# A decoder layer on one core: the scan's output projection as three products of split operands, its weight streamed

## The reference

```python
proj = hidden_states @ W_in.T
z, xBC, dt = split(proj)
xBC = silu(conv4(xBC) + conv_b)
dt = softplus(dt + dt_bias)
A_cum = cumsum(dt * -exp(A_log))
Lmat = exp(segsum(dA))
y = Y_diag + Y_off + D * x
g = y * silu(z)
gn = g * rsqrt(mean(g * g) + EPS) * norm_w
return gn @ W_out.T
```

## Time and profile before

| what | value |
|---|---|
| median of three runs | 1694.83 us |
| profiled execution, its own time | 1693.64 us |
| its span | 1691.9 us |
| TensorE matmul busy | 1603.2 us (95%) |
| VectorE busy | 1254.0 us (74%) |
| ScalarE busy | 1217.1 us (72%) |
| GpSimd busy | 731.8 us (43%) |
| mean DMA rate | 134 GB/s |

### The profile page before, as it was taken

One profiled execution on the slowest core, in us unless ns is written; L12 is line 12 of the kernel. 1 busy time (PEld: TensorE's weight loads), 2 busy tenths in 40 slices (PEclk: granted clock), 3 DMA queues, 4 the chain that ended last, 5 costly groups with the idle time before them and its releaser, 6 DMA issues. The chain is left out here.

```text
span 1691.9 us, 29098 instructions
## 1 busy us (share of the span) xinstructions
PE 1603.2 (95%) x9864; PEld 1281.0 (76%) x9864; DVE 1254.0 (74%) x2044; ACT 1217.1 (72%) x2518; POOL 731.8 (43%) x601
## 2 busy tenths in 40 slices
PE   5479999999999999999999999999969999999999
PEld 3357777777777777777777677878757889999888
DVE  7969999999999999999999865567666533333355
ACT  4679999999999999999999576566624324444331
POOL 1425555555555555555555511311113653334460
PEclk9689999999999999999999999999989999999999
DMA  8966444444444444444444100000215323222231
GB/s 324 389 231 253 164 152 172 150 158 167 151 172 152 154 171 150 173 151 153 172 150 150 55 1 13 14 14 14 72 75 190 117 96 133 90 91 95 79 99 51
DMA packets 78078, 226.62 MB, mean 134 GB/s; under 512 B 9072, under 2 KB 32880, under 8 KB 76272
## 3 DMA queue, kind: packets, MB, share of 16 engines
q1 hardware_dynamic: 72272, 198.67, 32.9%
q0 software_dynamic: 5664, 26.09, 4.4%
HBM read 187.77 MB, written 36.96 MB: 133 GB/s over the span
## 5 line engine op out<-in xcount | busy, mean ns | idle before, releaser
L776 DVE SCALAR_TENSOR_TENSOR m_xc<-banks,k_cw,m_xc 128x510 f32<-128x510 f32 (+2 forms) x384 | 285.4, 743 | 16.6 <-ACT m_xc L690 7.2
L917 PE MATMUL m_ps_out<-k_won,m_gT 128*128 128x256 f32 x1024 | 242.3, 379 | 3.2 <-POOL m_gT L640 2.0
L873 PE MATMUL banks<-pair_hi,m_wxz 128*128 128x512 f32 x680 | 241.7, 406 | 2.5 <-DMA m_wxz<-w_split 2.5
L640 POOL TENSOR_TENSOR m_gT<-m_gy,m_zs 128x512 f32<-128x512 f32 x128 | 166.4, 1300 | 172.3 <-DVE m_gy L817 171.4
L663 POOL TENSOR_TENSOR m_mat<-m_mat,k_cbm 128x384 f32<-128x384 f32 x128 | 129.8, 1014 | 230.6 <-DVE m_mat L789 216.8
L917 PEld LDWEIGHTS m_ps_out<-k_won,m_gT 128*128 128x128 f32 x1024 | 193.6, 190 | 36.1 <-POOL m_gT L640 3.3
L905 PE MATMUL m_ps_y<-m_mat,m_xdt 128*64 128x256 f32 (+1 forms) x2048 | 194.7, 332 | 0.0
L711 ACT ACTIVATE m_mat<-m_mat 128x1536 f32<-128x1536 f32 x128 | 188.6, 1473 | 0.0
L905 PEld LDWEIGHTS m_ps_y<-m_mat,m_xdt 128*64 128x64 f32 x2048 | 126.8, 136 | 80.0 <-issue 42.3
L702 ACT ACTIVATE m_mat<-m_a_all,k_cum 128x256 f32<-128x256 f32 x340 | 170.6, 502 | 0.0
L651 POOL TENSOR_TENSOR m_g_sum<-m_g_sum,m_g_sq 128x512 f32<-128x512 f32 x124 | 162.4, 1310 | 5.3 <-ACT m_g_sq L717 5.1
(11 more groups left out here) (325 smaller groups left out, 3774.9 us busy)
## 6 DMA issues: line engine op xcount, KB each, us to landing
m_wxz<-w_split SPq DMA_DIRECT2D x85, 512.0 KB, 3.4
m_a_all<-a_by_head SPq DMA_DIRECT2D x85, 512.0 KB, 4.4
k_w_first<-w_split SPq DMA_DIRECT2D x43, 512.0 KB, 3.3
k_a_first<-a_by_head SPq DMA_DIRECT2D x43, 512.0 KB, 4.2
w_split<-p_w_hl SPq DMA_DIRECT2D x15, 1024.0 KB, 8.6
raw<-in_w_gate_up POOLq DMA_DIRECT2D x9, 1280.0 KB, 6.5
raw<-in_w_xz SPq DMA_DIRECT2D x16, 512.0 KB, 7.1
raw<-in_w_down POOLq DMA_DIRECT2D x9, 640.0 KB, 7.9
```

The costliest lines, as they stand in the source:

```text
L640: pool.tensor_tensor(gT[:, n % 2, :], gy[:, n % 2, :], zs[:, n % 2, :], ALU.mult).then_inc(g_done, 1)
L776: dve.scalar_tensor_tensor(out=out[:, :, k:], in0=ps[:, :, 0:SEQ - k], scalar=cw[:, c, TAPS - 1 - k:TAPS - k], in1=out[:, :, k:], op0=ALU. ...
L873: last = pe.matmul(ps[:, :], w, a, start=m == 0, stop=m == len(terms) - 1)
L917: last = pe.matmul(ps_out[:, q * HID:(q + 1) * HID], gT[:, n % 2, q * P:(q + 1) * P], won[:, c, :], start=c == 0 and q % 2 == 0, stop=c == ...
```

## The change

The output projection no longer multiplies float32 operands. Each product g is split into a high part (`gT_hi`, ScalarE) and a low part (`gT_lo`, GpSimd) of type float32r, the output weight likewise (`won[..., 0]` and `won[..., 1]`), and `out_proj` issues three matmuls for each of the four token tiles: high x high, high x low, low x high, 12 in all. It runs one iteration later, for n-2 instead of n-1.

The output weight is no longer loaded in preparation. In the first group each tile of it is loaded (128 KB), multiplied by norm_w and rounded on ScalarE (`won_high`), its low part taken on VectorE (`won_low`), and the pair stored to DRAM (256 KB). In the later groups the pair is loaded again for each product, four buffers deep. All of that is issued by SyncE's queue (`move_won`).

One of the four pairs of `gaps` (head 1, sequence 1) moves from ScalarE to GpSimd (`pool_gaps`), three products ahead; `decays` now also waits for it. The sign that ScalarE took in `scale=-1.0` is now in the stored sums. Several semaphores are merged under new names (`x_silu` and `z_silu` to `silu_done` and so on), with counts to match.

```diff
-            def weigh_out(c):
-                if c == 0:
-                    act.wait_ge(wo_loaded, 16)
-                act.activation(won[:, c, :], won[:, c, :], ACT.Copy, scale=nw[:, c:c + 1]).then_inc(won_done, 1)
...
-            sp.dma_start(won[:], w_out).then_inc(wo_loaded, 16)
...
+            def move_won(n):
+                kept_c, c = n - WON - 2, n - WON
+                if n > WON:
+                    sp.wait_ge(won_moved, 16 * won_moves(n - 1))
+                if 0 <= kept_c < NCT:
+                    sp.wait_ge(won_lo_done, kept_c + 1)
+                    sp.dma_start(won_dram[kept_c], won[:, kept_c % WON].rearrange("p s m -> p (s m)").bitcast(F32))\
+                        .then_inc(won_moved, 16)
+                if 0 <= c < NCT:
+                    if c >= WON:
+                        sp.wait_ge(won_lo_done, c - WON + 1)
+                    sp.dma_start(won_raw[:, c % WON], w_out[:, c, :]).then_inc(won_moved, 16)
+                elif c >= NCT:
+                    sp.wait_ge(out_ready, c - WON + 1)
+                    sp.dma_start(won[:, c % WON].rearrange("p s m -> p (s m)").bitcast(F32), won_dram[c % NCT])\
+                        .then_inc(won_moved, 16)
...
-                    sp.wait_ge(gap_done, HPT * (n - 2))
+                    sp.wait_ge(exp_done, n - 2)
...
+            def low_part(n):
+                pool.wait_ge(gT_hi_done, n + 1)
+                if n >= 2:
+                    pool.wait_ge(out_ready, n - 1)
+                pool.tensor_tensor(gT_lo[:, n % 2, :], gT[:, n % 2, :], gT_hi[:, n % 2, :].bitcast(F32),
+                                   ALU.subtract).then_inc(gT_lo_done, 1)
...
+            def pool_gaps(n):
+                g, c, u = n // NCT, n % NCT, n % 3
+                pool.wait_ge(a_loaded[u], 16 * (n // 3 + 1))
+                if n >= 3:
+                    pool.wait_ge(y_ready, n - 2)
+                h, b = HPT - 1, BG - 1
+                head, t = c * HPT + h, g * TPG + 2 * b
+                pool.tensor_scalar(mat[:, u, h, b * TRI:b * TRI + SEQ], a_all[u][:, h, b * SEQ:(b + 1) * SEQ],
+                                   cum[:, t, head:head + 1], 0.0, ALU.add, ALU.max)
+                pool.tensor_scalar(mat[:, u, h, b * TRI + SEQ:(b + 1) * TRI],
+                                   a_all[u][:, h, b * SEQ + P:(b + 1) * SEQ],
+                                   cum[:, t + 1, head:head + 1], 0.0, ALU.add, ALU.max).then_inc(mat_pool, 1)
...
                     pool.wait_ge(mat_done, HPT * (n + 2))
                     last_matrix(n + 1)
+                if n >= 1:
+                    low_part(n - 1)
                 if n < N - 1:
                     product(n)
+                if n + 3 < N:
+                    pool_gaps(n + 3)
                 if n % NCT > 0:
                     add_square(n - 1)
...
-                for b in range(BG):
+                for b in range(BG - h):
...
             def decays(n):
                 act.wait_ge(gap_done, HPT * (n + 1))
+                act.wait_ge(mat_pool, pool_gap(n))
                 act.activation(mat[:, n % 3], mat[:, n % 3], ACT.Exp, scale=-1.0).then_inc(exp_done, 1)
+
+            def high_part(n):
+                act.wait_ge(g_done, n + 1)
+                if n >= 2:
+                    act.wait_ge(out_ready, n - 1)
+                act.activation(gT_hi[:, n % 2, :], gT[:, n % 2, :], ACT.Copy).then_inc(gT_hi_done, 1)
+
+            def won_high(c):
+                act.wait_ge(won_moved, 16 * won_moves(c + WON))
+                if c >= WON:
+                    act.wait_ge(out_ready, c - WON + 1)
+                act.activation(won[:, c % WON, 0], won_raw[:, c % WON], ACT.Copy, scale=nw[:, c:c + 1])\
+                    .then_inc(won_hi_done, 1)
...
-                if n == N - 1:
-                    wq_high()
-                if n >= 1:
-                    square(n - 1)
+                high_part(n - 1)
+                square(n - 1)
                 if n + 1 < N:
                     tanh_z(n + 1)
                 if n + 2 < N:
                     decays(n + 2)
+                if n <= NCT:
+                    won_high(n - 1)
+                if n == N - 1:
+                    wq_high()
+            high_part(N - 1)
             square(N - 1)
...
+            def won_low(c):
+                dve.wait_ge(won_hi_done, c + 1)
+                dve.scalar_tensor_tensor(out=won[:, c % WON, 1], in0=won_raw[:, c % WON], scalar=nw[:, c:c + 1],
+                                         in1=won[:, c % WON, 0].bitcast(F32), op0=ALU.mult, op1=ALU.subtract)\
+                    .then_inc(won_lo_done, 1)
...
                     silu_x(n + 1)
                     silu_z(n + 1)
+                if 1 <= n <= NCT:
+                    won_low(n - 1)
...
+                terms = [(gT_hi, 0), (gT_hi, 1), (gT_lo, 0)]
                 for q in range(TPG):
-                    last = pe.matmul(ps_out[:, q * HID:(q + 1) * HID], gT[:, n % 2, q * P:(q + 1) * P],
-                                     won[:, c, :], start=c == 0 and q % 2 == 0, stop=c == NCT - 1,
-                                     skip_group_check=True)
+                    for m, (a, part) in enumerate(terms):
+                        last = pe.matmul(ps_out[:, q * HID:(q + 1) * HID], a[:, n % 2, q * P:(q + 1) * P],
+                                         won[:, n % WON, part], start=c == 0 and q % 2 == 0 and m == 0,
+                                         stop=c == NCT - 1 and m == len(terms) - 1, skip_group_check=True)
```

162 lines of the change are left out of this document (95 added, 67 removed).

## The result

The changed kernel takes **1853.31 us** (median of four runs, 1852.20 to 1856.42) against 1694.60 us for the kernel before on the same chip: 1.0945 times as long, with a 95% interval of 1.0931 to 1.0958. The forecast was 1755, its range 1733 to 1788. The direction and both loops were right; the result lies 98 us above the forecast and 65 above the range.

The account below looks back on a forecast made before the run. The kernel was taken as bound by TensorE, 6.57 us per product. First group +40, groups two to four +20, preparation -1, tail +2 made +61 on 1693.64, 1754.6, given as 1755 us; range 1733 to 1788.

Parts of the forecast that it names:

- both loops: The first group's loop through `won_high` and `won_low`, 7.91 us, and the GpSimd-VectorE port loop in groups two to four, 6.78 us.
- the price g: GpSimd time for the two `pool_gaps` instructions per product: 0.72 us taken, from the copy's slope; high end 1.09.
- `pool_gaps` is dear: Rival, chance 0.17: at 1.09 us for the pair, groups two to four loop at 7.15, total 1790.
- the port loop: Groups two to four: GpSimd's instructions, then VectorE's L786 and L789; 6.06 + g, 6.78 us per product, +20 us in all.
- cover, not path: Groups two to four: the `gaps` pair leaving ScalarE runs while `conv_x` runs, so moving it shortens the ScalarE-VectorE chain by nothing.
- L786 records of 1.3 to 1.7 us: Sign in groups two to four: VectorE's L786 takes that long instead of 0.95 us.
- The 7.91 of the sum: First group: loop period in us through `conv_x`, ScalarE's work, `won_high` and `won_low`; 1.34 over the period, term +40 us.
- 6.04 + 0.52: ScalarE-VectorE chain, groups two to four: `high_part` adds 0.52 us, making 6.56 against 6.57, eating all that TensorE gives.
- The estimate of 1.31: TensorE: twelve isolated matmuls in 1.31 us by the skill's formula, 6.06 per product; the forecast used 1.63 and 6.38.
- The tail's +2: After the scan: `high_part` and a low part ahead of the last projection and sum, one more GpSimd instruction; 0.5 to 4.
- Preparation's -1: Before the scan: 4 MB of load and 13.2 us of ScalarE go, but only a 2.6 us queue wait can be saved.
- what would show it: Signs listed: first group's period 7.9 us, later groups 6.7 to 6.9, GpSimd busy nearly 5.5, `pool_gaps` 0.45 and 0.35.

Follow-up runs that it names:

- e1: Changed kernel plus fourteen GpSimd instructions ahead of the scan, seven forms at 128 and 256 columns; pointer add with max took 0.72 and 1.16 us.
- e9: Changed kernel plus seven more GpSimd tensor_scalar forms ahead of the scan, at 128 and 256 columns; pointer mult then constant add took 0.48 us, pointer max alone 0.92.
- e12: Changed kernel with both `pool_gaps` instructions as multiply by zero, then add a pointer scalar (that block's exponents not computed); 1780.95 us, ratio 1.0502.
- e10: Changed kernel with `pool_gaps` moved behind `add_square` in GpSimd's order, nothing added or removed; 1836.72 us, ratio 1.0853.
- e13: Order of e11, with the quick multiply-then-add form of `pool_gaps` in place of the memset (that block's exponents not computed); 1730.16 us, ratio 1.0204.
- e8: Changed kernel with the constant 1.0 replacing the pointer scalar in both `pool_gaps` instructions (that block's exponents not computed); 1792.35 us, one run.
- e2: Changed kernel with the fourth pair of `gaps` back on ScalarE; 1768.87 us, ratio 1.0442.
- e6: Changed kernel with `won_low` behind the next iteration's `x_times_dt` and a memset replacing `pool_gaps`' two tensor_scalar (exponents not computed); 1728.86 us, ratio 1.0196.
- e7: Kernel of e6 with `high_part` moved ahead of `tanh_x`; 1716.44 us, ratio 1.0123.
- e11: Kernel of e7 with `won_high` right behind `high_part`, `won_low` ahead of VectorE's `matrices`, the memset behind `add_square`; 1679.91 us, ratio 0.9928.

## Why the prediction was right or wrong

**Wrong: the price g.** The step is "the price g shows nowhere", with "I take 0.72, since `pool_gaps` has one tensor input, like the copy", and 1.09 as the high end. It is 1.80 uncontended. Both ends came from the number of inputs, the copy's slope and the two-input slope, but the number of inputs does not set the price of a tensor_scalar on GpSimd: the operations do (e1, e9). The start of 0.24 us was about right; what failed is the slope, 0.83 ns per column for a measured 3.4. Both "ends" are rows of other operations, and such rows do not bound anything. One row was also missed: the trace before has a GpSimd tensor_scalar of 8 columns in preparation (L240, 0.272 and 0.318 us) beside the one of 4 columns (0.240), two additions like it, which already rises by more than the copy's slope. The rival "`pool_gaps` is dear", 0.17, was the right one, its 1790 too low. e12 shows that this one price, with the waiting that it brings, is most of the error: with 0.80 us in that place the ratio is 1.0502, which is 1780 on 1694.6, and 73 of the 98 us are gone. The Trainium skill (GPSIMD Engine Reference, "Elementwise — side-by-side cycle accounting") has 1.8 cycles per element as the best loop, which the prediction turned into g = 0.98; the trace does not agree, with 3.4 ns per column for this form and 0.9 for the quick one.

**Wrong in part: the port loop's form, and a wait put at nothing.** With g = 1.80, 6.06 + g is 7.86; 7.63 is measured, and the loop is another one. The sum took it that only the four two-input instructions meet at the port, and it called the pair of `gaps` that leaves ScalarE "cover, not path". But `pool_gaps` itself is held, for 1.1 us behind L856 and L859, and `decays` waits 0.94 us for it. So the pair is on the path: port, `pool_gaps`, `decays`, `scale_x`, `conv_x`, L856 and L859, 7.62 us around. That loop is read from the trace's waits; no run took the wait of `decays` away alone, but e10 and e13 fit it. "L786 records of 1.3 to 1.7 us" was not seen in groups two to four (L856 1.02) and is no longer expected there; in e12, where g was small, it was (1.89). In e8, where L859 is held by `add_square` in some stretches, the pace is 7.25.

**Right: two loops, each with its place.** The wait before `won_low` for `won_high` is there, though with 0.39 us and not the 1.1 that were forecast, since L859 is held by `add_square` before it. The 7.91 of the sum is short of 8.49 by 0.58, and 0.53 of that is what `won_low` waits for `low_part` (1.01 against 0.48): "the port loop with `won_low` added is 7.05 and hides beneath it" overlooked that the port also lengthens the chain above it. In e2 and e12, where `low_part` is out of the way, the first group runs at 7.95 and 7.99. Its term was 40; e12 has 37 for it, and the change 51.

**Right: ScalarE's and VectorE's chain.** 6.04 + 0.52 was the reason to say that the split gives nothing by itself; e6 runs at 6.57. Taking `high_part` out of it (e7 against e6) gave 12 us. In groups two to four it gave 633.1 - 623.8 = 9.3, where 9 was expected.

**Right, and a little pessimistic: TensorE.** Twelve matmuls took 604.40 - 602.78 = 1.62 us in the change (1.63 forecast), 1.51 where they were not waiting for anything (e11: 203.12 - 201.60 = 1.52), so TensorE's own period is 6.27 and not 6.38. The estimate of 1.31 by the Trainium skill (TensorE: Matmul & The Clock Gate, "Back-to-back issue gap") is not reached in any run; the shortest is 1.51. The forecast's remark that all loops must be under it to gain was borne out by e11.

**Small terms.** The tail's +2 is +3.1. Preparation's -1 is +6.1: GpSimd's program does `pool_gaps(0)` to `(2)` ahead of the first `last_matrix`, and the second and third wait there for their sums to load (3.76 and 0.68 us). With the pair on ScalarE (e2) the first `last_matrix` starts at 98.84. That was in the code and was not counted.

**Of "what would show it"**: the first group's wait (but not its size), a period over 7.5 and TensorE's idle time held; `pool_gaps` at 0.45 and 0.35 did not, and it was the line that would have told at once. GpSimd shows no gap, where 5.5 us of each period were forecast; its work is 6.5 us, and the rest is held time.

## What to carry to other kernels

A price for which the trace has no row of the same operation is bounded by other operations only if something says that the operation doesn't matter; otherwise the high end stays open, and the forecast should say what the answer is at two and three times the price. Where two engines share a port, add up for each of them the time of all its instructions there and look at who arrives first, since the wait lands on whichever is late, and a small instruction (0.46 us in e13) can wait longer than it works. An engine without a gap need not be the bound, as a held instruction counts as busy: follow the waits of the other engines until they close. Before moving work to an engine that is 43% busy, place it where the others leave that engine idle: the same split, in another order and with the one slow pair left out uncomputed, went from 9% slower to 0.7% faster (e11).

## What the runs showed of the hardware that was not expected

- GpSimd's tensor_scalar on 256 fp32 columns: 0.42 to 0.48 us for a multiplication followed by an addition, 0.92 to 1.21 for every other combination tried.
- A GpSimd tensor_scalar with a pointer scalar waits for VectorE's two-input instructions, through both of them (L706: 2.23 us in the change, 1.58 in e13). With a constant it works meanwhile and ends with the second of them at the latest (e8: one L708 started at 458.04, 0.01 us behind L856, and took 1.43 us, up to L859's end at 459.46, instead of 0.65). A memset is never held (e11: 0.41 to 0.45 us in all 128). Where it comes first, it holds VectorE only a little: in e10 L706 started at 200.32, L856 at 200.47 and took 1.13 us against 0.95; in the change, 0.08 us behind L706, 1.21. What in the pointer form waits, the reading of the pointer perhaps, was not separated.
- VectorE's tensor_scalar with a single SBUF input is held by GpSimd's two-input instructions (1.36 and 1.32 us beside them, 0.41 and 0.27 alone). The Trainium skill (SBUF — State Buffer, "Who interferes with whom") says that tensor_scalar can enter a mode with both ports and then contends; the trace agrees with the contention, and shows nothing of the mode.
- The same program settles at two paces, 7.25 and 6.58 us per product within one run of e8, with the engines in another order at the port.
